# Two-layer graph network: projections as plain fp32 matmuls of unsplit operands instead of three fp32r matmuls of split ones

## The reference

```python
q, k, v = heads(x @ Wq + bq), heads(x @ Wk + bk), heads(x @ Wv + bv)      # 6 heads of 64
probs = softmax(q @ k.T / 8 + where(adj, 0, -9e15))
x = layernorm(x + (probs @ v) @ Wf + bf)

h = einsum('bnd,ade->bane', x, W)                                        # 12 heads of 32
th = tanh(h)
attn = leaky_relu(th @ w_src + (th @ w_dst).T, 0.2)
attn = softmax(where(adj, attn, -999))
f = elu(attn @ h + b)
gate = sigmoid(x @ H_w.T + H_b)
x = layernorm(x + gate * f + (1 - gate) * x)
```

## Time and profile before

| | |
|---|---|
| median of 3 runs | 1132.66 us (1132.14 to 1134.66) |
| the profiled execution | 1132.1 us, of which the span of the trace is 1130.2 us |
| mean granted clock of TensorE | 0.986 |
| busy: PE, PEld | 95%, 78% |
| busy: DVE, ACT, POOL | 79%, 81%, 68% |

### The profile page before, as it was taken

The page is one execution under the profiler, slowest core; times in us unless marked ns, Lnnn a source line. Parts: engine busy times, 40 slices in busy tenths (PEclk is TensorE's granted clock), DMA queues, the critical chain, the costliest instruction groups (busy, mean ns, idle before and its releaser), DMA issues.

```text
span 1130.2 us, 25501 instructions
## 1 busy us (share of the span) xinstructions
PE 1073.2 (95%) x8236; PEld 883.3 (78%) x8236; DVE 897.2 (79%) x1828; ACT 919.4 (81%) x3383; POOL 765.2 (68%) x909
## 2 busy tenths in 40 slices
PE   6889999999999999999999999999999999997774
PEld 5678888888888888878888888888888888786652
DVE  5457878888887888888788888878888887888874
ACT  3348888888888888888888888888888888888874
POOL 1367776676777667677766767776676777667652
PEclk9999999999999999999999999999999999999986
DMA  9101010020101002010100201010020101000000
GB/s 270 56 2 57 15 68 18 8 71 16 64 15 61 26 8 71 16 64 15 62 26 8 71 15 64 15 60 27 8 72 16 64 15 43 16 8 16 16 15 21
DMA packets 25893, 44.66 MB, mean 40 GB/s; under 512 B 2462, under 2 KB 23714, under 8 KB 25762
## 3 DMA queue, kind: packets, MB, share of 16 engines
q1 hardware_dynamic: 23234, 41.91, 10.9%
q10 hardware_dynamic: 2496, 1.12, 0.5%
q0 software_dynamic: 32, 0.00, 0.0%
HBM read 30.43 MB, written 12.58 MB: 38 GB/s over the span
## 4 chain that ended last, share of the span: by engine, by line
PE 57%; POOL 23%; issue 9%; DVE 6%; ACT 3%; DMA 2%; POOLq 0%; ACTq 0%; DVEq 0%
PE ps_b L253 13%; PE ps_d L253 13%; POOL z L964 9%; PE ps_a L253 7%; PE ps_d L459 5%; POOL xT_lo L916 4%; PE ps_a L382 3%; PE ps_s L362 3%; PE ps_s L354 3%; PE ps_d L447 3%; POOL p L991 3%; PE ps_c L469 2%; POOL s L956 2%; POOL thw L999 2%; POOL y L958 2%
## 5 line engine op out<-in xcount | busy, mean ns | idle before, releaser
L583 ACT ACTIVATE z<-z,s 128x128 f32<-128x128 f32 x768 | 297.1, 391 | 1.5 <-DVE s L798 0.9
L964 POOL TENSOR_TENSOR z<-z,mask 128x512 f32<-128x512 f32 x192 | 218.2, 1164 | 0.5 <-ACT z L679 0.5
L583 ACT ACTIVATION_READ_ACCUMULATOR z<-z,s 128x1 f32 x768 | 146.6, 191 | 0.0
L610 ACT ACTIVATE p<-ps_s,s 128x128 f32<-128x128 f32 x384 | 134.7, 378 | 13.1 <-DVE s L776 13.0
L991 POOL TENSOR_TENSOR p<-p,s 128x768 f32<-128x768 f32 x64 | 94.2, 1471 | 61.4 <-DVE s L804 61.4
L459 PE MATMUL ps_d<-ident,z 128*128 128x128 f32 x768 | 118.7, 278 | 9.2 <-ACT z L583 8.2
L953 POOL TENSOR_SCALAR s<-s 128x1 f32<-128x1 f32 x128 | 28.8, 225 | 143.3 <-DVE s L895 131.6
L999 POOL TENSOR_TENSOR thw<-th,w_sd 128x768 f32<-128x768 f32 x64 | 117.4, 1834 | 3.7 <-ACT th L633 3.7
L459 PEld LDWEIGHTS ps_d<-ident,z 128*128 128x128 f32 x768 | 90.6, 143 | 17.6 <-ACT z L583 9.1
L679 ACT ACTIVATE z<-ps_d 128x512 f32<-128x512 f32 x192 | 100.8, 598 | 1.2 <-PE ps_d L447 1.2
L945 POOL TENSOR_TENSOR xb<-xb,bf_all 128x768 f32<-128x768 f32 x32 | 58.6, 1834 | 58.6 <-DVE sd L878 55.5
(11 more groups left out here) (154 smaller groups left out, 3448.5 us busy)
## 6 DMA issues: line engine op xcount, KB each, us to landing
x_cols<-in_xT_dram SPq DMA_DIRECT2D x16, 768.0 KB, 6.4
xb<-in_x_dram SPq DMA_DIRECT2D x16, 768.0 KB, 4.9
out_dram<-y SPq DMA_DIRECT2D x64, 192.0 KB, 1.8
z<-in_L_gnn_Wq_dram SPq DMA_DIRECT2D x1, 576.0 KB, 6.4
p1T<-in_L_gnn_Wk_dram SPq DMA_DIRECT2D x1, 576.0 KB, 8.7
qT<-in_L_gnn_Wv_dram SPq DMA_DIRECT2D x1, 576.0 KB, 11.1
kT<-in_L_gnn_Wf_dram SPq DMA_DIRECT2D x1, 576.0 KB, 13.4
z<-in_L_gnn_W_dram SPq DMA_DIRECT2D x1, 576.0 KB, 11.7
```

Of the source, the lines that this page charges most:

```text
L583: done = act.activation(z[:, a, :], z[:, a, :], ACT.Exp, bias=neg1[:, a:a + 1], accum_out=sum1[:, a:a + 1])
L610: last = act.activation(p0[:, o, i, :], ps_s[:, o, i * N:(i + 1) * N], ACT.Exp, bias=neg0[:, k:k + 1], accum_out=sum0[:, k:k + 1])
L964: pool.tensor_tensor(z[:, 4 * q:4 * q + 4, :], z[:, 4 * q:4 * q + 4, :], mask[:, t, :].unsqueeze(1).broadcast_to([P, 4, N]), ALU.add).then ...
```

## The change

Every projection becomes one plain fp32 matmul per chunk, on operands that are kept once. The parts, the copies that make high parts of x and of the weights, and all subtractions go. The copies of x1T and ctxT from PSUM stay, with fp32 output. x is loaded straight into one half of a double buffer `xT`, and each weight straight into its own buffer. The semaphores follow; products that waited for a low part wait for the copy or for the DMA.

```diff
-        w_parts = {n: [sb(f"{n}_hi", [P, C, D], F32R), sb(f"{n}_lo", [P, C, D], F32R)]
-                   for n in ("wq", "wk", "wv", "wf", "w1", "hw")}
+        weights = {n: sb(n, [P, C, D]) for n in ("wq", "wk", "wv", "wf", "w1", "hw")}
-        x_cols = sb("x_cols", [P, C, G * N])
-        xT = [sb("xT_hi", [P, C, G * N], F32R), sb("xT_lo", [P, C, G * N], F32R)]
+        xT = sb("xT", [P, 2, C, G * N])
-        ctxT = [sb("ctxT_hi", [P, C, N], F32R), sb("ctxT_lo", [P, C, N], F32R)]
+        ctxT = sb("ctxT", [P, C, N])
-        x1T = [sb("x1T_hi", [P, C, N], F32R), sb("x1T_lo", [P, C, N], F32R)]
+        x1T = sb("x1T", [P, C, N])
...
-            sp.dma_start(x_cols[:], xT_in[0]).then_inc(S["x_in_ready"], 16)
+            sp.dma_start(xT[:, 0, :, :], xT_in[0]).then_inc(S["x_even_in"], 16)
-                if n >= 4:
-                    sp.wait_ge(S["weight_lo"], n - 3)
-                sp.dma_start(stage[n % 4], DRAM_W[name].rearrange("(c p) n -> p c n", p=P)
+                sp.dma_start(weights[name][:], DRAM_W[name].rearrange("(c p) n -> p c n", p=P)
                              ).then_inc(S[f"weight_in_{n}"], 16)
...
-                    if n == 0:
-                        sp.wait_ge(S["x_lo_first"], 2)
-                    else:
-                        sp.wait_ge(S["x_lo"], xb_and_x_lo)
-                    sp.dma_start(x_cols[:], following).then_inc(S["x_in_ready"], 16)
+                    if g > 0:
+                        sp.wait_ge(S["v_made"], G * g)
+                    sp.dma_start(xT[:, 1 - par, :, :], xT_in[g + 1]).then_inc(S["x_odd_in" if g % 2 == 0 else "x_even_in"], 16)
...
-            def split_product(out_ap, lhs, rhs, chunks=range(C), closed=True):
+            def product(out_ap, lhs, rhs, chunks=range(C), closed=True):
 
                 for c in chunks:
-                    for k, (a, b) in enumerate(HI_LO):
-                        last = pe.matmul(out_ap, lhs(a, c), rhs(b, c), start=(c == 0 and k == 0),
-                                         stop=(closed and c == C - 1 and k == 2))
+                    last = pe.matmul(out_ap, lhs(c), rhs(c), start=(c == 0), stop=(closed and c == C - 1))
                 return last
...
                 for c in range(C):
-                    for k in range(2):
-                        last = pe.matmul(ps_s[:, 0, 0:D], bv_col[:, c:c + 1].broadcast_to([P, P]),
-                                         w_parts["wf"][k][:, c, :].bitcast(F32), start=(c == 0 and k == 0),
-                                         stop=(c == C - 1 and k == 1))
+                    last = pe.matmul(ps_s[:, 0, 0:D], bv_col[:, c:c + 1].broadcast_to([P, P]),
+                                     weights["wf"][:, c, :], start=(c == 0), stop=(c == C - 1))
...
-                        act.activation(x1T[0][:], ps_b[:, 0:D].rearrange("p (c n) -> p c n", c=C),
-                                       ACT.Copy).then_inc(S["x1_hi"], 1)
+                        act.activation(x1T[:], ps_b[:, 0:D].rearrange("p (c n) -> p c n", c=C),
+                                       ACT.Copy).then_inc(S["x1T_ready"], 1)
-                    if qkv and n + 1 < NG and j == 3:
-                        x_hi(g + 1, 0)
...
-                        act.activation(ctxT[0][:], ps_a[:, 0:D].rearrange("p (c n) -> p c n", c=C),
-                                       ACT.Copy).then_inc(S["ctx_hi"], 1)
+                        act.activation(ctxT[:], ps_a[:, 0:D].rearrange("p (c n) -> p c n", c=C),
+                                       ACT.Copy).then_inc(S["ctx_ready"], 1)
...
-                    if gat:
-                        lo_part(x1T, ps_b, slice(0, N), "x1_hi", tl + 1, "x1_lo")
...
-                    if att:
-                        dve.wait_ge(S["ctx_made"], ta + 1)
-                        lo_part(ctxT, ps_a, slice(0, N), "ctx_hi", ta + 1, "ctx_lo")
...
-                    if qkv and n + 1 < NG and j == 3:
-                        x_lo(g + 1, 0)
-                        x_lo(g + 1, 1)
```

More of the change, by code:

```diff
@@ L394, in project_out @@
                         pe.wait_ge(S["r0_ready"], t)
-                    pe.wait_ge(S["ctx_lo"], t + 1)
+                    pe.wait_ge(S["ctx_ready"], t + 1)
                     if n == 1 and j == 0:
-                        pe.wait_ge(S["weight_lo"], 4)
-                last = split_product(ps_b[:, 0:D], lambda a, c: ctxT[a][:, c, :],
-                                     lambda b, c: w_parts["wf"][b][:, c, :], chunks)
+                        pe.wait_ge(S["weight_in_3"], 16)
+                last = product(ps_b[:, 0:D], lambda c: ctxT[:, c, :], lambda c: weights["wf"][:, c, :], chunks)
                 if chunks[-1] == C - 1:
@@ L416, in project_h @@
                 if isinstance(t, int) and t == 0:
-                    pe.wait_ge(S["weight_lo"], 6)
+                    pe.wait_ge(S["weight_in_4"], 16)
+                    pe.wait_ge(S["weight_in_5"], 16)
                     pe.wait_ge(S["hb_moved"], 16)
                     pe.wait_ge(S["pick_ready"], 2)
-                split_product(ps_d[:, 1, 0:D], lambda a, c: x1T[a][:, c, :],
-                              lambda b, c: w_parts["w1"][b][:, c, :]).then_inc(S["h_made"], 1)
+                product(ps_d[:, 1, 0:D], lambda c: x1T[:, c, :],
+                        lambda c: weights["w1"][:, c, :]).then_inc(S["h_made"], 1)
             def project_gate(chunks):
-                split_product(ps_d[:, 2, 0:D], lambda a, c: x1T[a][:, c, :],
-                              lambda b, c: w_parts["hw"][b][:, c, :], chunks, closed=False)
+                product(ps_d[:, 2, 0:D], lambda c: x1T[:, c, :],
+                        lambda c: weights["hw"][:, c, :], chunks, closed=False)
                 if chunks[-1] == C - 1:
@@ L542, in _ @@
             act.activation(bq8[:], bq_col[:], ACT.Copy, scale=D0 ** -0.5).then_inc(S["bias_ready"], 1)
[L544 to L548, removed]
-                    act.wait_ge(S["v_made"], G * (g - 1) + 2 * (half + 1))
-                act.activation(xT[0][:, :, at], x_cols[:, :, at], ACT.Copy).then_inc(S["x_hi"], 1)
-            x_hi(0, 0)
-            x_hi(0, 1)
-            for n in range(3):
-                act.wait_ge(S[f"weight_in_{n}"], 16)
-                act.activation(w_parts[W_ORDER[n]][0][:], stage[n], ACT.Copy).then_inc(S["weight_hi"], 1)
             act.wait_ge(S["bias_ready"], 1)
@@ L637, in iteration @@
                         evacuate_v(2)
-                    if qkv and n + 1 < NG and j == 3:
-                        x_hi(g + 1, 1)
                     if att:
@@ L692, in _ @@
             dve.wait_ge(S["bias_ready"], 1)
-            for half in range(2):
-                at = slice(2 * half * N, 2 * (half + 1) * N)
-                dve.wait_ge(S["x_hi"], half + 1)
-                dve.tensor_tensor(xT[1][:, :, at], x_cols[:, :, at], xT[0][:, :, at].bitcast(F32), ALU.subtract
-                                  ).then_inc(S["x_lo_first"], 1)
-            def weight_parts(n):
-                hi, lo = w_parts[W_ORDER[n]]
-                if n < 3:
-                    dve.wait_ge(S["weight_hi"], n + 1)
-                else:
-                    dve.wait_ge(S[f"weight_in_{n}"], 16)
-                    dve.tensor_copy(hi[:], stage[n % 4]).then_inc(S["late_hi"], 1)
-                    dve.wait_ge(S["late_hi"], n - 2)
-                dve.tensor_tensor(lo[:], stage[n % 4], hi[:].bitcast(F32), ALU.subtract).then_inc(S["weight_lo"], 1)
             def small_constants():
@@ L731, in small_constants @@
                 dve.tensor_copy(hb_split[:, 2, :], hb_rest[:, 1, :]).then_inc(S["hb_small"], 1)
-            for n in range(3):
-                weight_parts(n)
             def iteration(g, par, n):
                 qkv, att = parts(n)
-                def lo_part(parts_, source, at, name_hi, count, name_lo):
-                    dve.wait_ge(S[name_hi], count)
-                    dve.tensor_tensor(parts_[1][:, :, at], source[:, 0:D].rearrange("p (c n) -> p c n", c=C),
-                                      parts_[0][:, :, at].bitcast(F32), ALU.subtract).then_inc(S[name_lo], 1)
                 def evacuate_q(m):
@@ L853, in iteration @@
                         evacuate_v(3)
-                    if n == 0 and j < 3:
-                        weight_parts(3 + j)
                     if n == 0 and j == 3:
@@ L911, in _ @@
         def _(pool):
-            def x_lo(g, half):
-                at = slice(2 * half * N, 2 * (half + 1) * N)
-                pool.wait_ge(S["x_hi"], 2 * g + half + 1)
-                pool.tensor_tensor(xT[1][:, :, at], x_cols[:, :, at], xT[0][:, :, at].bitcast(F32), ALU.subtract
-                                   ).then_inc(S["x_lo"], 1)
             pool.memset(minus_half[:], -0.5)
```

65 lines of the change are left out of this document (27 added, 38 removed).

## The result

The changed kernel takes 1243.1 us (median of 4 runs, 1241.88 to 1243.56), the kernel before 1132.4 us beside it: 1.0971 times as long, with a 95% interval of 1.0952 to 1.099.

A forecast was written before the change was run, and what follows sets the result against it. PE's queue without holes was taken to bound the middle, latency between engines the ends. Fourteen groups at 8.0 us (112) plus 1 + 5 + 3.5 made 121.5 us, hence 1254 us; own range 1246 to 1263, 8 in 10 1242 to 1270.

The forecast's parts named there:

- the fourteen groups: Steady loop between ramp and tail: 8.95 us dearer chunks less 0.9 us relief, 8.0 us per group, 112 us in all.
- start and ramp: First two groups: about +1 us net for the first, +5 us for the second (ends 2 and 7.5).
- the tail: Last steps, without fills: dearer chunks and two last h products at a falling clock, +3.5 us, ends 0 and 6.
- Rival 4: PE's entries into small blocks get cheaper too, or ramp and tail absorb all; some 1240 us or less, chance 0.04.
- The bound: From 100 to 1050 us PE's queue has no holes, so every nanosecond added to its stream shows in the time.
- The price of a chunk: One fp32 matmul per chunk in PE's projections: 0.645 us at 384 columns (before 0.521), 0.86 at 512 (before 0.693).
- Rival 2: PE's fp32 matmul of ordinary operands costs two column times, L328 being a special case; some 1045 us, chance 0.04.
- rival 3: A real chunk in PE's loop costs 8% more, 0.69 and 0.92 us, adding 55 us; some 1305 us, chance 0.06.
- Rival 1: All 288 chunks of 512 and 768 of 384 columns cost full price without relief; some 1270 us, chance 0.10.
- The relief: In the loop, the 0.13 us hole before the logits fills each step and POOL's lateness goes: 0.9 us per group.
- the late POOL: First step of each group: POOL's x subtractions make it reach the scaling late; removing them saves 0.4 us per group.
- The circle: In steps without fills, a 15.0 us chain through all engines; five PE chunks on it add 0.6 us for four steps.

## Why the prediction was right, point by point

**The number.** 1243.1 us lies in the range given for 8 in 10 (1242 to 1270), at its very edge, and below the forecast's own range of 1246 to 1263. The sum was too high by 10.8 us, and all its parts erred to the same side: the fourteen groups by 4.7, start and ramp by 2.2, the tail by 4.0. Rival 4, 1240 us because entries into small blocks get cheaper or the ends absorb all, was nearer in its number and partly came true: the ends cost 3.3 us of the 9.5 counted, and a step grew a little less than its sum.

**The bound.** Right. PE's queue is full from 100 us to the tail in both kernels, and the matmuls alone give the loop its length: the same 17.77 us with the side work and without it.

**The price of a chunk.** Right, 0.645 and 0.86 us, as L328 and the scaling by columns gave them. Rival 2 (two column times) and rival 3 (8% more in the loop) fall by the same rows: 1.94 and 2.58 us for a block in the loop. Rival 3's own sum, 1253.6 + 55, makes 1309 and not 1305. Rival 1, the full price and no relief at 1270 us, is answered by the run that keeps all the relieved work and still takes only 1254.

**The loop.** 107.3 us against 112. Each step came out 0.09 us shorter than its sum: +1.90 where 6 x 0.167 + 9 x 0.124 - 0.13 = 1.99 were worked out. No single term carries the difference. From the starts in both traces the two Q or K blocks grew by 0.97 us instead of 1.00 (the run with Q and K alone says the same), the h block by 0.35 instead of 0.37 (it took 1.59 us before, not the 1.56 of the V block that I had used), the gate chunks by 0.36 instead of 0.37, and the first two out chunks with the hb row ahead of them by 0.22 instead of 0.25. So the chunk of before was a little dearer in the loop than in the blocks that I read it from. Whether it is the entry into these chunks that was dearer is read off starts, not tested.

**The relief.** Right in size for the late POOL: 5.3 us measured without the dearer matmuls against 5.6. With them it is worth less, 2.9 us with all the other relief in the loop, since the longer queue covers most of it. For the logits 0.11 us were covered against 0.13; but the place held another 0.14 us of order that the change left untouched, which I had not seen.

**The start and ramp.** +3.8 us against +6. The first mask came at +0.4 instead of +1, by two errors that cancel. The first group's fills cost 5.1 us more and not 4.5 (7.83 to 33.24 against 11.12 to 31.47), since the first block was slow. DVE's small constants ran 1.3 us faster: the copy to cols_R took 0.42 us where it had taken 1.76 beside POOL's subtraction. The second group cost +3.4 instead of +5, inside its ends.

**The tail.** -0.5 us against +3.5, the sign wrong. The circle grew by 0.51 to 0.57 us in each of four steps, as worked out (0.6). But for the last two h products I added cost at a falling clock, and in the step of the first of them the clock did not fall:

```profile
1178.35:1193.47 15.12, 11.87 (x85) 7.31 (x84) 12.01 (x26) 13.19 (x51) 9.52 (x13) 1.00 0.04 15
1193.47:1206.66 13.19, 8.89 (x60) 4.94 (x60) 9.01 (x19) 10.26 (x37) 8.69 (x13) 1.00 0.04 16
```

The second of these steps took 14.12 us at 0.88 before, and 13.19 at 1.00 now; what follows it took 35.9 us at 0.67 before and 34.2 at 0.70 now. Together that is 2.6 us off, against 2.2 us more in the four steps ahead. Part of it is luck of the two executions traced: two runs with the matmuls of before in their tail also show 13.2 us at 1.00 for this step. More work for PE alone does not keep the clock either: the changed kernel with the mask first has the same projections in its tail and ran three steps at 0.90.

**The rivals' time.** Rival 2's 1045 us was not tested. The run with a single fp32r product has less work for PE than its chunks and still took 1126 us, but it keeps POOL's subtractions in its chain, which rival 2's kernel would not have. At full clock its second step took the 14.92 us that rival 2 reckoned with, its fourth 16.43. How much of the rest is the clock and how much POOL's work was not separated.

## What to carry to other kernels

Before replacing three cheap matmuls by one dear one, look for any instruction of the dear kind in the trace, however marginal, and take its start-to-start time: six matmuls of a bias product gave the price of a chunk to within 1%. The time of the change came out 10% smaller than worked out, from many small terms at the ends and entries. Work taken off the engines beside a full queue is worth its share of the ramp and of the few steps where it arrives late, here 11 of 122 us. Where PE's queue and a chain through the other engines are almost equally long, taking matmuls away wins little: here two thirds of the projections' matmuls were worth 7 us, with PE pausing a quarter of the time at a mean clock of 0.92. A clock seen in one trace is no property of the kernel; look for the same stretch in a run that did not touch it.

## What the runs showed of the hardware that I had not expected

- A DVE subtraction of 128x768 took 0.956 us with POOL idle, 2.22 us in the 14 cases in which a POOL subtraction had started 0.4 us before it, and 0.95 us in the one case in which POOL's operation started after it; there POOL's operation took 2.40 us, and the next one of its kind 1.84. A copy to cols_R of 64x512 took 0.42 us alone and 1.76 us when a POOL subtraction had started 0.3 us before it. So who starts first seems to decide who loses; for the second order this rests on a single case.
- A step without fills took 15.0 us at a granted clock of 1.00 and 16.6 us at 0.90 with nearly the same instructions. It was seen at 0.90 in the three kernels with the mask first and no added matmuls and in the one without low parts; in the other kernels, with one product apart, the first three of these steps all ran at 1.00. What decides it is open.
- Two bf16 mask matmuls placed ahead of the bf16 logits instead of behind them shortened a step by 0.14 us in a kernel that had no hole left there to fill. Why is open.
